# An RWKV, attention and MXINT8 decoder layer on one core: quantised operands turned by DMA instead of TensorE, the bias of the first FFN layer added while its result is read out, four jobs moved to ScalarE, and every order written anew

## The reference

```python
# 32 sequences of 128 tokens, width 512, f32; ln = layernorm without weights
def attn(x):                      # RWKV-5, 32 heads of 16, two chunks of 64
    xx = shifted(x) - x           # x one token earlier, minus x
    r, k, v = (x + xx*maa_r) @ Wr.T + br, (x + xx*maa_k) @ Wk.T + bk, (x + xx*maa_v) @ Wv.T + bv
    g = silu((x + xx*maa_g) @ Wg.T + bg)
    y = decayed_linear_attention(r, k, v, exp(-exp(time_decay)), time_faaaa)
    return (norm_per_head(y) * ln_g + ln_b) * g @ Wo.T + bo
def xattn(q, kv):                 # 32 query heads, 8 key and value heads of 16; kv = ctx for both
    return softmax(q @ kv.T / 4) @ kv
def ffn(x):                       # quant: MXINT8, a shared exponent for each 32 values of a row
    h = bf16(bf16(norm(bf16(x))) * ln_w + ln_b)
    h = bf16(gelu(bf16(quant(h) @ quant(W1).T + b1)))     # 512 -> 2048
    return bf16(bf16(x) + bf16(quant(h) @ quant(W2).T + b2))   # 2048 -> 512
x = x + attn(ln(x)); x = x + xattn(ln(x), ctx); x = x + ffn(ln(x))
```

## Time and profile before

| | before |
|---|---|
| median of 3 runs | 1512.8 us (1510.5 to 1513.35) |
| the profiled execution's own time | 1516.44 us |
| its span, first to last instruction | 1513.7 us |
| granted TensorE clock, mean | 0.979 |
| PE busy | 1367.1 us (90%) |
| DVE busy | 1256.8 us (83%) |
| ACT busy | 750.9 us (50%) |
| POOL busy | 571.5 us (38%) |
| chain that ended last, share by PE / DVE | 84% / 7% |

### The profile page before, as it was taken

How to read it: one execution, slowest core, us unless ns; L and a number is a source line. 1 busy time by engine, 2 the same in 40 slices (tenths; PEclk the granted TensorE clock), 3 DMA queues, 4 the chain that set the end, 5 groups by cost and what they waited for, 6 DMA issues and landing times.

```text
span 1513.7 us, 31642 instructions
## 1 busy us (share of the span) xinstructions
PE 1367.1 (90%) x12356; PEld 890.6 (59%) x12448; DVE 1256.8 (83%) x2066; ACT 750.9 (50%) x1367; POOL 571.5 (38%) x607
## 2 busy tenths in 40 slices
PE   0177899999999999999999999999999999999764
PEld 0056656666666666666666666666666666666422
DVE  3687878888888888888888889888888888988753
ACT  0313445555555455555555545555555545555552
POOL 2254433444443333344444343333444433333221
PEclk9998999999999999999999999999999999999977
DMA  6111100000000000000000000000000000000000
GB/s 251 68 31 52 38 11 17 9 18 18 10 18 18 17 17 17 18 16 10 18 10 18 18 17 18 17 18 17 9 18 15 13 18 18 17 17 11 8 8 14
DMA packets 48673, 36.63 MB, mean 24 GB/s; under 512 B 35584, under 2 KB 37008, under 8 KB 47888
## 3 DMA queue, kind: packets, MB, share of 16 engines
q1 hardware_dynamic: 48528, 34.62, 8.0%
HBM read 25.68 MB, written 8.39 MB: 23 GB/s over the span
## 4 chain that ended last, share of the span: by engine, by line
PE 84%; DVE 7%; issue 3%; DMA 2%; ACT 2%; SPq 1%; POOL 1%; POOLq 0%; DVEq 0%; ACTq 0%
PE bank_b L325 14%; PE bank_y L362 7%; PE bank_y L444 7%; PE bank_a L315 7%; PE bank_a L325 7%; PE rt L383 5%; PE rt L335 4%; PE rt L396 4%; PE bank_o L402 4%; PE bank_y L348 4%; PE bank_a L426 4%; PE bank_b L426 4%; DMA gmem<-w 2%; PE bank_o L356 2%; PE rt L373 2%
## 5 line engine op out<-in xcount | busy, mean ns | idle before, releaser
L3028 POOL TENSOR_TENSOR x<-x,o_bf 128x512 f32<-128x512 f32 x32 | 37.0, 1158 | 419.3 <-DVE o_bf L1554 419.3
L1400 DVE TENSOR_TENSOR att<-rt,wm 128x2048 f32<-128x2048 f32 x64 | 146.6, 2291 | 11.8 <-PE rt L335 9.8
L1444 DVE TENSOR_REDUCE negm<-rt 128x16 f32<-128x2048 f32 x64 | 146.3, 2286 | 7.0 <-PE rt L383 6.9
L3023 POOL TENSOR_TENSOR gmem<-gmem,unit_g 128x1024 bf16<-128x1024 bf16 x64 | 122.8, 1919 | 20.6 <-DVE unit_g L1499 20.6
L325 PEld LDWEIGHTS bank_b<-mix_k,w_Wk 128*128 128x128 f32 x1024 | 119.3, 192 | 15.4 <-issue 14.8
L2990 POOL TENSOR_SCALAR mix_r<-xx,all_columns 128x128 f32<-128x128 f32 x128 | 54.1, 438 | 191.4 <-DVE xx L1358 191.4
L325 PE MATMUL bank_b<-mix_g,w_Wg 128*128 128x128 f32 x1024 | 125.3, 282 | 0.0
L1488 DVE TENSOR_REDUCE amax_g<-gmem 128x32 f32<-128x1024 bf16 x64 | 77.7, 1215 | 55.6 <-ACT gmem L2444 55.5
L2415 ACT ACTIVATE pT<-rt 128x2048 f32<-128x2048 f32 x64 | 119.6, 1869 | 7.4 <-PE bank_o L402 4.6
L444 PE MATMUL bank_y<-w2q,gmem 128*128 128x512 bf16 x480 | 115.2, 395 | 7.7 <-ACT gmem L2450 5.8
L362 PE MATMUL bank_y<-w_Wo,yT 128*128 128x512 f32 x256 | 118.3, 605 | 4.0 <-DVE yT L1421 3.9
(11 more groups left out here) (192 smaller groups left out, 3005.1 us busy)
## 6 DMA issues: line engine op xcount, KB each, us to landing
xin<-x SPq DMA_DIRECT2D x32, 256.0 KB, 2.7
gmem<-w SPq DMA_DIRECT2D x16, 512.0 KB, 3.6
out<-x SPq DMA_DIRECT2D x32, 256.0 KB, 2.1
kv<-ctx SPq DMA_DIRECT2D x32, 64.0 KB, 2.6
w_Wv<-Wv SPq DMA_DIRECT2D x1, 1024.0 KB, 5.5
w_Wk<-Wk SPq DMA_DIRECT2D x1, 1024.0 KB, 8.1
w_Wr<-Wr SPq DMA_DIRECT2D x1, 1024.0 KB, 11.2
w_Wg<-Wg SPq DMA_DIRECT2D x1, 1024.0 KB, 13.4
```

The costliest lines, as they stand in the source:

```text
L1400: e.tensor_tensor(att[:, :, :, :, :].rearrange("p g m a t -> p (g m a t)"), rt[:, :], wm[:, i, :, :, :, :].rearrange("p g m a t -> p (g m ...
L1444: e.tensor_reduce(negm[:, 0:H].rearrange("p (g i j) -> p g i j", g=4, i=2)[:, :, i, :], rt[:, :].rearrange("p (g j s) -> p g j s", g=4, j= ...
L3023: e.tensor_tensor(blocks(half), blocks(half), per_block(unit[f"g{i}"], 32), ALU.mult).then_inc(sem(f"pool_gsc{i}"), 1)
```

## The change

It does these things:

- `turn_hidden`, `turn_gelu` and `turn_w12` go from PE, and `hidden_turned`, `gelu_turned` and `copy_w12` from ACT. In their place SP issues DMAs with transpose=True, SBUF to SBUF: one for the hidden values of a sequence, one for each half of gelu's result, and for each piece of W1 two, of W2 one. `up` and `down` wait for these DMAs.
- The three-row matmul of `up` goes, with `b1_in_parts` and `b1_rows`. b1 is loaded as f32 into all partitions (1 MB), and `up_out` moves to DVE, where it adds it. z_bf has two buffers.
- `normalise_q`, `normalise_x` and `normalise_f` move to ACT as scale * x + bias, where the bias is -mean * rstd: DVE negates the mean (one 128x1 instruction), ACT multiplies (another). `receptance` moves to ACT as eight 128x128 pieces. DVE's `shift` is now called `differences`.
- All orders are new. `bonuses`, all quantisation but `w12_quantise(15)` and all 16 `w12_scaled` now stand ahead of sequence 0.

```diff
+            def w12_turned(n):
+                e.wait_ge(sem("dve_w_q"), n + 1)
+                k, half = n // 2 % 4, n % 2
+                if n < 8:
+                    for a in range(2):
+                        at = (4 * k + 2 * half + a) * P
+                        e.dma_start(w1q[:, :, at:at + P], wq[n % 2][:, a * C:(a + 1) * C],
+                                    transpose=True).then_inc(sem(f"sp_wT{n % 2}"), 16)
+                else:
+                    e.dma_start(w2q[:, 8 * half:8 * half + 8, k * P:(k + 1) * P], wq[n % 2],
+                                transpose=True).then_inc(sem(f"sp_wT{n % 2}"), 16)
+            def hidden_turned(n):
+                e.wait_ge(sem("dve_hq"), n + 1)
...
+                e.dma_start(hqT[:, :, :], h_bf, transpose=True).then_inc(sem("sp_hqT"), 16)
+            def gelu_turned(n, i):
+                e.wait_ge(sem(f"dve_gq{i}"), n + 1)
+                if n:
+                    e.wait_ge(sem("pe_down"), n)
+                e.dma_start(gqT[:, 8 * i:8 * i + 8, :], g_bf[:, 2 * C * i:2 * C * (i + 1)],
+                            transpose=True).then_inc(sem(f"sp_gqT{i}"), 16)
...
             def up(n, j, bank):
-                e.wait_ge(sem("act_hqT"), n + 1)
+                e.wait_ge(sem("sp_hqT"), 16 * (n + 1))
...
-                e.matmul(bank[:, :], ones[32 * j:32 * j + 3, :], b1rows[32 * j:32 * j + 3, :], start=True, stop=False)
                 for c in range(KT):
                     done = e.matmul(bank[:, :], hqT[:, c, :], w1q[:, c, j * C:(j + 1) * C],
-                                    start=False, stop=(c == KT - 1))
+                                    start=(c == 0), stop=(c == KT - 1))
...
             def down(n):
-                e.wait_ge(sem("act_gqT0"), n + 1)
-                e.wait_ge(sem("act_gqT1"), n + 1)
+                e.wait_ge(sem("sp_gqT0"), 16 * (n + 1))
+                e.wait_ge(sem("sp_gqT1"), 16 * (n + 1))
...
+            def up_out(n, j, bank):        # on DVE
+                e.wait_ge(sem(f"pe_z{j}"), n + 1)
...
+                e.scalar_tensor_tensor(z_bf[j % 2], bank[:, :], 0.25, b1row[:, j * C:(j + 1) * C], ALU.mult,
+                                       ALU.add).then_inc(sem(f"dve_ze{j}"), 1)
...
+            def normalise_q(n):            # on ACT
...
+                e.activation(xn, xin[n % 2][:, :], ACT.Identity, bias=shift["q"][:, 1:2],
+                             scale=rstd["q"][:, 0:1]).then_inc(sem("act_xn"), 1)
...
+            def receptance(n):
...
+                for m in range(KT):
+                    for a in range(2):
+                        done = e.activation(rz[:, m, a, :], bank_a[:, m * T:(m + 1) * T], ACT.Identity,
+                                            bias=br_of[:, a, m:m + 1], scale=parity[:, a:a + 1])
...
-            for n in range(8, 27):
...
+            for n in range(11, 30):
+                e.wait_ge(sem("dve_x1"), n - 3)
+                down(n - 7)
```

More of the change, by code:

```diff
@@ new lines, in _ @@
+            stats_g(1)
+            maxima(2, 1)
+            gate_in(3)
+            norm_mv("g", 1)
+            gelu_max(0, 1)
+            gate(3)
+            gelu_pow2(0, 1)
+            decayed(3, 1)
+            weighted(1)
+            mixed(4, "v")
+            gelu_round(0, 0)
+            hidden(1)
+            hidden_max(1)
+            hidden_pow2(1)
+            scaled_y(3)
+            gelu_round(0, 1)
+            gated_y(3)
+            hidden_scale(1)
+            hidden_round(1)
@@ L1911, in _ @@
+            mixed(7, "v")
+            gelu_round(3, 0)
+            stats_g(4)
+            norm_mv("g", 4)
+            weighted(4)
+            gelu_round(3, 1)
+            hidden(4)
+            hidden_max(4)
+            hidden_pow2(4)
+            scaled_y(6)
+            gated_y(6)
+            hidden_scale(4)
+            hidden_round(4)
+            gelu_quantised(3, 1)
+            hidden_quantised(4)
             gelu_quantised(3, 0)
-            gelu_pow2(3, 1)
+            first_sum(6)
@@ new lines, in _ @@
+            norm_mv("g", 5)
+            weighted(5)
+            hidden(5)
+            hidden_max(5)
+            hidden_pow2(5)
+            scaled_y(7)
+            gated_y(7)
+            hidden_scale(5)
+            for n in range(11, 30):
+                gelu_round(n - 7, 1)
+                hidden_round(n - 6)
+                gelu_round(n - 7, 0)
+                hidden_quantised(n - 6)
+                gelu_quantised(n - 7, 0)
+                gelu_quantised(n - 7, 1)
+                first_sum(n - 4)
+                stats_x(n - 4)
+                spread_v(n - 3)
+                norm_mv("x", n - 4)
+                up_out(n - 6, 1, bank_b)
+                stats_q(n - 2)
+                norm_mv("q", n - 2)
+                decayed(n - 3, 0)
+                second_out(n - 7)
+                residual(n - 7)
+                up_out(n - 6, 0, bank_a)
+                differences(n - 2)
+                mixed(n - 2, "k")
+                up_out(n - 6, 3, bank_b)
+                denominators(n - 5, 1)
+                normalise_o(n - 5, 1)
+                up_out(n - 6, 2, bank_a)
+                denominators(n - 5, 0)
+                normalise_o(n - 5, 0)
+                maxima(n - 4, 1)
+                gelu_max(n - 6, 0)
+                stats_f(n - 5)
+                maxima(n - 4, 0)
+                gate_in(n - 3)
+                norm_mv("f", n - 5)
+                gate(n - 3)
+                gelu_pow2(n - 6, 0)
+                decayed(n - 3, 1)
+                gelu_max(n - 6, 1)
+                gelu_pow2(n - 6, 1)
+                mixed(n - 2, "v")
+                stats_g(n - 5)
+                norm_mv("g", n - 5)
+                weighted(n - 5)
+                hidden(n - 5)
+                hidden_max(n - 5)
+                hidden_pow2(n - 5)
+                scaled_y(n - 3)
+                gated_y(n - 3)
+                hidden_scale(n - 5)
@@ L2560, in _ @@
-            up_out(0, 3, bank_b)
-            gelu(0, 3)
-            squares(3)
             e.preload_act_table_set(TABLE_EXP)
             rstd_log("f", 1)
+            rstd_exp("f", 1)
+            normalise_f(1)
+            e.preload_act_table_set(TABLE_GELU)
+            gate_tanh(3)
+            maxima_turned(2)
+            e.preload_act_table_set(TABLE_EXP)
+            rstd_log("g", 1)
+            receptance(4)
+            squares(3)
+            keys_r(4)
             head_log(3)
+            rstd_exp("g", 1)
@@ new lines, in _ @@
+            queries_x(6, 0)
+            queries_x(6, 1)
+            gate_tanh(7)
+            gelu(4, 3)
+            gelu(4, 2)
+            e.preload_act_table_set(TABLE_EXP)
+            rstd_log("f", 5)
+            maxima_turned(6)
+            rstd_exp("f", 5)
+            receptance(8)
+            normalise_f(5)
+            squares(7)
+            keys_r(8)
+            rstd_log("g", 5)
+            head_log(7)
+            rstd_exp("g", 5)
+            head_rstd(7)
+            weights_x(6, 0)
```

2864 lines of the change are left out of this document (1286 added, 1578 removed).

## The result

The changed kernel takes 1535.9 us (median of 4 runs, 1531.3 to 1538.0), the kernel before 1513.1 in the same session: a ratio of 1.014, with a 95% interval of 1.010 to 1.018. The change costs 23 us. The forecast was 1457, its range ended at 1530, and the chances put 0.77 on faster.

A forecast was written before the change was run, and what follows sets the result against it. It took the steady part to be bound by PE (TensorE) and nearly nothing else. Start 118 + ramp 321.5 + 22 periods of 39.5 + end 149 = 1457.5, less 0.9 and rounded: 1457 us, range 1438 to 1530.

The forecast's parts named there:

- PE's relief: Each sequence on PE: turns and bias matmuls go, 2.67 us less, giving a PE-bound period of 39.2.
- DVE's sum: Steady period on DVE: loses 4.1 us of work, gains 3.1, so 1.0 less, 35.8 of 39.2 us.
- The price of a turning DMA: SP's queue: a turned half costs a plain issue, 0.6 us, the lower end of the bounds.
- rival A: Steady part: turning DMAs hold SP's queue, 2.3 us a half; turning point about 2.1; 1523 us, chance 0.20.
- the upper bound: SP's queue pushing each 128x128 block separately: 5.0 us for a half, 2.5 for the hidden values.
- rival C: Transfers land 1 us later than plain ones, making the last half and x late: 1484 us, chance 0.12.
- x behind the turns: Steady part: the next x is ready for turn_x at about 16.6 to 16.9, wanted at 16.6; 0.3 us a period charged.
- Rival B: Steady part: PE and DVE, both full, wait for each other, 0.8 us a period; 1479 us, chance 0.20.
- The start: Before the first turn_x: nine pieces 46 us, bonuses 8.5, less stall 9, b1 1.2, earlier work 5; +39.5, to 118.
- beyond 130, turns hold the loads: Sign at the start: a first turn_x beyond 130 us would say that turns hold the pieces' loads.
- The ramp: First nine turn_x intervals: 353 us fall by 33 to 320, plus 0.3 x 5, hence 321.5.
- The end: After the last turn_x: 161 us become 149, by -11 PE's relief, +3 DMAs, -4 work side by side.

The follow-up runs named there:

- e6: The kernel before without its four bias matmuls a sequence, b1 left out of the output; 1477.5 us, 0.9769.
- e10: The kernel before without its bias matmuls and with three turning matmuls a sequence instead of twenty, one block copied to all places; 1451.3 us, 0.9588.
- e2: The changed kernel with the turning DMAs of hidden and gelu values replaced by plain DMAs of the same bytes; 1510.9 us, 0.9966.
- e1: The changed kernel with a third buffer for x, each x asked for one period earlier; 1520.4 us, 1.0032 of the kernel before.
- e5: The changed kernel with weight pieces 7 to 15 and bonuses spread over the first sequences and a third buffer for x; 1470.3 us, 0.9719.
- e3: The changed kernel with the turning DMAs of the sixteen weight pieces replaced by plain ones; 1532.3 us, 1.0106.
- e4: The changed kernel with weight pieces 7 to 15 and bonuses moved from ahead of sequence 0 to between the first sequences' instructions; 1491.9 us, 0.9831.
- e9: e5 with the last two sequences' work in another order on DVE, ACT and SP; 1470.2 us, 0.9708.
- e12: e9 with the last sequence's up halves 2 and 3 ahead of down(30), and its quantisation ahead of second_out(30); 1461.2 us, 0.9644.
- e11: e5 with ACT's first cross-attention exponential moved ahead of the two logarithms and the head's rate; 1479.2 us, 0.9765.

## Why the prediction was wrong, step by step

**What bounds the kernel: right.** e6 took out 1.24 us of PE's work, by the earlier trace rows, and the period fell by 1.22; e10's PE ran for 400.00 of 400 us.

**PE's relief: oversized.** 2.67 us a sequence was forecast; e6 and e10 give 1.22 + 0.87 + an estimated 0.15 = 2.24. The 0.13 for a bias matmul's wait does not count, and 17 of the 20 turns, priced from the start-to-start times in the earlier trace rows at 1.10, were worth 0.87. That is 0.4 of the 1.44 us.

**DVE's sum: wrong in sign.** DVE should have worked 1.0 us less a period. In 400 us it worked 363.47, so 37.2 in 40.94, where the earlier trace rows give 36.8. One cause is what POOL does beside DVE. Before, its scaling of gelu ran beside `gated_y`, and its mixing of r beside `mixed(n, "v")`; `mixed(n, "k")` had POOL idle beside it. Now the mixing of r runs beside k and the scaling beside v. Four like groups of DVE, before and then now, and POOL's scaling:

```profile
727.30 1.48 DVE L1365 SCALAR_TENSOR_TENSOR mix_v<-xx,all_columns,xT 128x128 f32<-128x128 f32 x4
...
736.87 1.12 DVE L1365 SCALAR_TENSOR_TENSOR mix_k<-xx,all_columns,xT 128x128 f32<-128x128 f32 x4
```

```profile
749.54 1.48 DVE L1304 SCALAR_TENSOR_TENSOR mix_k<-xx,all_columns,xT 128x128 f32<-128x128 f32 x4
...
766.46 2.79 DVE L1304 SCALAR_TENSOR_TENSOR mix_v<-xx,all_columns,xT 128x128 f32<-128x128 f32 x4
```

```profile
766.62 1.95 POOL L2875 TENSOR_TENSOR gmem<-gmem,unit_g 128x1024 bf16<-128x1024 bf16 x1 [1.05 <-DVE unit_g L1411]
```

So k went from 1.12 to 1.48 and v from 1.48 to 2.79, while `gated_y` lost the 0.97 forecast (1.66 to 0.69): together 0.7 more a period. The forecast took the stretch out of `gated_y` and put it nowhere. What DVE's longer work cost the kernel by itself, no run shows.

**The price of a turning DMA: between the bounds, and both ends of the reasoning missed it.** I took 0.6 us of SP's queue, rival A 2.3. Measured: 1.26 for a half and 1.23 for the hidden values, which are half as large. So it is not a price by the block, as the upper bound had it, nor is it the plain one. In all the turning of the steady values cost 25 us (e2), near the 27 of rival C, which had a chance of 0.12. The 1.7 us a half, estimated from the Trainium skill's "DMA: Bandwidth & Descriptors", and 2.2 with its fixed part, went by the tile, and 1.26 and 1.23 do not bear it out. The Trainium skill's "Advanced Engine Details and Errata", section X-Bar Transpose (TRN2), calls such DMAs as fast as regular ones; here a half lands after 3.2 us where a plain one of the same bytes lands after 2.3, and holds the queue 1.26 where that one holds it 0.48. The measurement decides. The 1309 ns that the Trainium skill's "VectorE: DVE Perf Modes", section The three transpose paths, gives for one block is near what issuing a DMA of four or of eight blocks takes here; it does not add up block by block.

**x behind the turns: right mechanism, small error.** 0.3 us a period were charged, e1 gives 0.42 in the mean and 0.6 in most periods. Rivals A and C are both partly true and neither decides: A's turning point of 2.1 us was not reached, and C's second half lands 0.9 late. What `down` and others lose to turns beyond x is e1 against e2, 40.52 - 40.25 = 0.27. That one is weak: each figure is of one execution, most periods of e1 are as short as e2's (40.16), the mean difference comes from single ones of 41.0, and e5, with e1's steady part, has 40.31, only 0.06 above e2.

**Rival B: true, at about its price.** With plain DMAs the period is 40.25, and PE alone would need an estimated 39.6; its busy time in the changed kernel says the same, 387.30 / 400 x 40.94 = 39.6. Of the 0.65 between, 0.39 is the wait for ACT's exponential; the other 0.26 I can't lay at one place. The kernel before had neither. So the 1.44 us of the steady part are 0.40 relief, 0.12 x, 0.27 other turns, 0.39 ACT and 0.26 that are the rest, not measured by themselves.

**The start: the term that failed is what was taken off, the 15.2 us for the stall.** (9 for the stall, 1.2 for the parts of b1, 5 for work that already stood in it.) The two kernels can be compared where eight pieces are scaled and seven quantised; `means_removed`, 6.5 us, is left out. Before that is at 75.59 - 6.5 = 69.1, in the changed kernel at 68.45: of the 15.2 us only 0.6 came. From there to the statistics of sequence 0, at 131.00, pass 62.6 us. Without `means_removed` and the 8.4 of `bonuses` these are 47.6 for the added pieces, against 46 forecast. So "about 10.2 a pair" held in the sum, with single pairs from 9.3 (behind `means_removed` or `bonuses`, under which their loads land) to 13.6, and some 14.5 of the 15.9 us are the deduction. Rows of DVE: the end of piece 4 before, then now, piece 7's scale and the end of piece 6 now:

```profile
45.93 1.22 DVE L1571 SCALAR_TENSOR_TENSOR hz<-gmem,pow_w 128x1024 bf16<-128x1024 f32 x1
```

```profile
50.72 1.23 DVE L1494 SCALAR_TENSOR_TENSOR hz<-gmem,pow_w 128x1024 bf16<-128x1024 f32 x1
...
63.34 1.22 DVE L1482 TENSOR_REDUCE amax_w<-gmem 128x32 f32<-128x1024 f32 x1 [2.33 <-DMA gmem<-w]
...
68.45 0.68 DVE L1490 TENSOR_SCALAR gmem<-gmem 128x1024 f32<-128x1024 f32 x1
```

By the end of piece 4 the changed kernel is 4.8 us late, and from there it gains 5.4, not 15.2: the wait of 9.01 became one of 2.33, not none. Its loads land after 4.5 us instead of 3.6. Later, both buffers come free together, and DVE stands for a load at the pair of pieces 10 and 11:

```profile
90.29 1.22 DVE L1482 TENSOR_REDUCE amax_w<-gmem 128x32 f32<-128x1024 f32 x1 [4.09 <-DMA gmem<-w]
```

e3 shows that at most 3.2 us of the start are the turning. Why the loads take longer, no run shows. The sign "beyond 130, turns hold the loads" in my forecast was a wrong reading of a right number. Worse is what I did not ask: whether the pieces need stand there at all. The forecast's own cover, the 38 us that DVE sheds in the ramp, was room that DVE had to spare, and e4 takes 44 us back by using it again.

**The ramp:** 327.0 against 321.5, near the forecast.

**The end: a gain that was mostly not there.** I expected -11 us from PE's relief, -4 from evacuations side by side and +3 for the DMAs. Without the bias (e6) the end takes 155.7 us and with few turns too (e10) 158.3, against 161.0 before: 3 to 5 us for all of PE's relief. The new order with plain DMAs needs 170.0, with turning ones 174.6. So 4.6 us are the turns' and some 12 to 14 those of the rest of the change, of the order, the moved work and the plain DMAs in PE's place together, which no run parts. How much an order can be worth there e9 and e12 show: they took back 8 us of the end by order alone (e5: 1466.7 - 1293.3 = 173.4; e12: 1460.2 - 1295.0 = 165.2). PE's clock is lower there too: between 1400 and 1440 us its mean is 0.79 of the full 2.4 GHz in the changed kernel, 0.94 before, between the two levels of 1.2 and 2.4 GHz, after waits of 2.4 and 2.2 us for DVE's maxima and decay; before, then now:

```profile
1400.00:1440.00 40.00, 30.30 (x273) 16.47 (x277) 30.09 (x49) 21.47 (x36) 9.78 (x7) 0.94 0.02 8
```

```profile
1400.00:1440.00 40.00, 30.46 (x249) 16.60 (x250) 26.96 (x46) 17.58 (x31) 10.79 (x8) 0.79 0.13 27
```

How much of the longer end is the clock's and how much the waits' was not taken apart.

## What to carry to other kernels

Work off the critical engine is free only where that engine has work. Moving nine pieces of weight preparation and the decay masks ahead of the first sequence cost 44 us although it removed as much DVE work from the stretch behind it; place such work by what stands idle there. A DMA's price is its landing and also its hold on the queue: ask what stands behind it, and give that another buffer before touching the DMA. And in an order without slack a wait that is taken away can come back as others, and more of them (e11); a relief came out at about its full size where nothing else stood close behind the bound (e6, e10).
